# Layer 2's second block of gates and binary products as three rounded products each

## The reference, cut to what matters

```python
xn = _layernorm(x, axis=-1)
# L2_attn
i_raw, f_raw, g = xn @ Wi, xn @ Wf, xn @ Wg
i = silu(i_raw) * sigmoid(-f_raw)
a = exp(log_sigmoid(f_raw))
o = scan(a, i)                      # o[t] = a[t] * o[t-1] + i[t]
o = o * rsqrt(mean(o * o) + EPS) * g_norm_weight * silu(g)
# L2_ffn
bw = where(w >= 0, 1, -1) * mean(abs(w), per output row)
x = x + o @ Wo + xn @ bw.T + bias
```

## Time and profile before

| what | value |
|---|---|
| median of three runs | 674.25 us |
| the profiled execution's own time | 672.19 us |
| its span, first to last instruction | 670.4 us |
| TensorE matmul busy | 640.1 us, 95% |
| VectorE busy | 535.0 us, 80% |
| ScalarE busy | 344.5 us, 51% |
| GpSimd busy | 336.5 us, 50% |
| granted TensorE clock | 1.00 in every slice |

### The profile page before, as it was taken

The page is one execution under the profiler, slowest core; times in us unless marked ns, Lnnn a source line. Parts: engine busy times, 40 slices in busy tenths (PEclk is TensorE's granted clock), DMA queues, the critical chain, the costliest instruction groups (busy, mean ns, idle before and its releaser), DMA issues. The chain is left out here.

```text
span 670.4 us, 13518 instructions
## 1 busy us (share of the span) xinstructions
PE 640.1 (95%) x4850; PEld 502.5 (75%) x4850; DVE 535.0 (80%) x1080; ACT 344.5 (51%) x749; POOL 336.5 (50%) x267
## 2 busy tenths in 40 slices
PE   8998999999899999999999999999999999999887
PEld 3446887788478988889898788888877756767666
DVE  4378777698699898889899998668456889889993
ACT  1596211400556576664657555576436474379641
POOL 1063555592357667474875737978519633220000
PEclk9999999999999999999999999999999999999999
DMA  8801000000601001010010101100422200100001
GB/s 262 348 0 65 2 1 1 2 0 0 243 17 42 24 8 39 16 39 23 25 36 10 39 16 42 52 30 27 154 67 61 70 3 0 40 0 1 2 0 64
DMA packets 14792, 31.38 MB, mean 47 GB/s; under 512 B 1853, under 2 KB 8603, under 8 KB 14173
## 3 DMA queue, kind: packets, MB, share of 16 engines
q1 hardware_dynamic: 13069, 27.25, 12.1%
q0 software_dynamic: 1536, 3.15, 1.7%
q10 hardware_dynamic: 144, 0.40, 0.3%
HBM read 26.59 MB, written 5.24 MB: 47 GB/s over the span
## 5 line engine op out<-in xcount | busy, mean ns | idle before, releaser
L625 PE MATMUL bank<-zone 128*128 128x256 f32 (+1 forms) x472 | 166.8, 353 | 9.0 <-DVE arena L1778 2.7
L627 PE MATMUL bank<-zone 128*128 128x256 f32 (+1 forms) x472 | 156.1, 331 | 0.0
L626 PE MATMUL bank<-zone 128*128 128x256 f32 (+1 forms) x472 | 156.1, 331 | 0.0
L625 PEld LDWEIGHTS bank<-zone 128*128 128x128 f32 x472 | 88.7, 188 | 33.8 <-issue 12.2
L2274 POOL TENSOR_TENSOR arena<-arena 128x512 f32<-128x512 f32 x64 | 82.2, 1285 | 61.7 <-ACT arena L1351 61.6
L2279 POOL TENSOR_TENSOR arena<-arena 128x512 f32<-128x512 f32 x64 | 84.3, 1317 | 23.4 <-DVE arena L1778 13.0
L627 PEld LDWEIGHTS bank<-zone 128*128 128x128 f32 x472 | 88.8, 188 | 9.0
L626 PEld LDWEIGHTS bank<-zone 128*128 128x128 f32 x472 | 89.0, 189 | 5.3
L1370 ACT ACTIVATE arena<-arena 128x256 f32<-128x256 f32 (+1 forms) x128 | 62.1, 486 | 29.2 <-DVE arena L1787 28.6
L1787 DVE CUSTOM_DVE_ANT_0 arena<-bank,const 128x256 f32<-128x256 f32 (+1 forms) x128 | 45.6, 403 | 18.5 <-PE bank L821 17.5
L1803 DVE SCALAR_TENSOR_TENSOR x<-bank,arena,x 128x256 f32<-128x256 f32 x128 | 53.0, 473 | 7.7 <-PE bank L627 7.1
(11 more groups left out here) (299 smaller groups left out, 1340.2 us busy)
## 6 DMA issues: line engine op xcount, KB each, us to landing
arena<-in_qk SPq DMA_DIRECT2D x16, 256.0 KB
arena<-in_tern SPq DMA_DIRECT2D x1, 3072.0 KB, 20.9
arena<-in_wv SPq DMA_DIRECT2D x8, 256.0 KB, 2.8
arena<-in_wo SPq DMA_DIRECT2D x16, 128.0 KB, 2.0
arena<-in_wr SPq DMA_DIRECT2D x1, 1792.0 KB, 9.2
lB<-in_lB SPq DMA_DIRECT2D x1, 1288.5 KB, 23.6
xg_rows<-arena SPq DMA_DIRECT2D x1, 1024.0 KB
arena<-in_cossin SPq DMA_DIRECT2D x2, 512.0 KB, 4.7
```

Of the source, the lines that this page charges most:

```text
L625: pe.matmul(dst, lhi, rhi, start=(n == 0), stop=False)
L626: pe.matmul(dst, lhi, rlo, start=False, stop=False)
L627: last = pe.matmul(dst, llo, rhi, start=False, stop=(n == len(terms) - 1 and not open_end))
```

## The change

In layer 2, the six gate groups of block 1 and the binary products of token pairs 2 and 3 are computed as split products. Block 0 keeps its fp32 products.

- ScalarE gets a rounded copy of the three gate weights at once (128x1536) ahead of the ternary weights, and a rounded copy of bwT (128x512) ahead of the plain one. Its two copies of block 1's transposed tiles are rounded and go to xT3 and no longer to xT.
- VectorE gets two subtractions (rests of block 1, from PSUM) ahead of `recurrence(0)`, each behind a wait for ScalarE's copy. They give the semaphore on which TensorE's gates of block 1 wait.
- GpSimd gets four rests of 128x512: one of the gate weights ahead of the power of block 0, two behind it, and the one of bwT behind the power of block 1, ahead of the bias addition.
- TensorE waits for the rests of the weights (`rests2`) ahead of block 1's gates and ahead of the binary products of pairs 2 and 3.
- The arrays wg2 and bwT2 lie in memory of layer 1 that is no longer used. Two semaphores are new, two unused ones are gone.

```diff
+        bwT2 = [Carve(zone, z.at + 2 * BW + n * KD * D).grid(KD, D) for n in range(2)]
+        wg2 = [Carve(zone, ZONE - 6 * KD * D - 128 + n * 3 * KD * D).cols(3 * KD * D) for n in range(2)]
...
             def gate2(n, half, b):
-                base = B_W + (1, 0, 2)[n] * KD * D + half * P
-                wide(g_gate2[n][half][b], lambda k: lB[:, base + k * D:base + k * D + P], xT, b)
+                base = (1, 0, 2)[n] * KD * D + half * P
+                if b == 0:
+                    wide(g_gate2[n][half][b], lambda k: lB[:, B_W + base + k * D:B_W + base + k * D + P], xT, b)
+                    return
+                g = g_gate2[n][half][b]
+                reuse(g)
+                split_product(g.ps, [(cut(parts(wg2), ALL, slice(base + k * D, base + k * D + P)), cut(parts(xT3), ALL, k, slice(BW, T)))
+                                     for k in range(KD)]).then_inc(g.full_sem, 1)
...
             def project_ffn2(p):
-                tall(g_ffn2[p], p, lambda t: [(xT[:, k, tok(t)], bwT[:, k, :]) for k in range(KD)])
+                if p < 2:
+                    tall(g_ffn2[p], p, lambda t: [(xT[:, k, tok(t)], bwT[:, k, :]) for k in range(KD)])
+                    return
+                g = g_ffn2[p]
+                reuse(g)
+                for tt in range(2):
+                    last = split_product(g.ps[:, tt * D:(tt + 1) * D], [(cut(parts(xT3), ALL, k, tok(2 * p + tt)), cut(parts(bwT2), ALL, k)) for k in range(KD)])
+                last.then_inc(g.full_sem, 1)
...
                 pe.wait_ge(xT_ready, 4 * KD + KD * (b + 1))
+                if b:
+                    pe.wait_ge(rests2, 3)
...
             turn_ternary(range(4, len(g_wT3)))
+            pe.wait_ge(rests2, 4)
...
+            act.activation(wg2[0].bitcast(F32R), lB[:, B_W:B_W + 3 * KD * D], ACT.Copy).then_inc(rounded2, 1)
             keep_ternary(range(3))
             keep_xT(2, [0])
             keep_ternary([3])
             act.wait_ge(*g_bwT.full)
+            act.activation(bwT2[0].bitcast(F32R), g_bwT.ps.rearrange("p (k o) -> p k o", k=KD), ACT.Copy).then_inc(rounded2, 1)
             act.activation(bwT, g_bwT.ps.rearrange("p (k o) -> p k o", k=KD), ACT.Copy).then_inc(g_bwT.ready_sem, 1)
...
                         if (n, half, b) == (2, KD - 1, 0):
-                            keep_xT(2, [1])
+                            for k in range(KD):
+                                act.wait_ge(*g_xT[2][1][k].full)
+                                act.activation(xT3[0][:, k, BW:T].bitcast(F32R), g_xT[2][1][k].ps, ACT.Copy).then_inc(rounded2, 1)
...
+            for k in range(KD):
+                dve.wait_ge(rounded2, k + 3)
+                dve.tensor_tensor(xT3[1][:, k, BW:T].bitcast(F32R), g_xT[2][1][k].ps, xT3[0][:, k, BW:T], ALU.subtract).then_inc(xT_ready, 1)
             recurrence(0)
...
-            inverse_deviations(2)
-
+            def rest_of_wg2(n):
+                at = slice(n * KD * D, (n + 1) * KD * D)
+                rest([t[:, at] for t in wg2], lB[:, B_W + n * KD * D:B_W + (n + 1) * KD * D]).then_inc(rests2, 1)
+
+            pool.wait_ge(rounded2, 1)
+            rest_of_wg2(0)
+            inverse_deviation(2, 0)
+            rest_of_wg2(1)
+            rest_of_wg2(2)
+            inverse_deviation(2, 1)
+
+            pool.wait_ge(rounded2, 2)
+            pool.wait_ge(*g_bwT.ready)
+            rest(bwT2, bwT).then_inc(rests2, 1)
             pool.wait_ge(xn_ready, 3 * NT)
             pool.wait_ge(bias2_loaded, 16)
             pool.tensor_tensor(x, x, bias2.unsqueeze(1).to_broadcast([P, NT, D]), ALU.add).then_inc(bias2_added, 1)
```

More of the change, by code:

```diff
@@ L228, in build @@
         osq_summed = sem("osq_summed")
+        rounded2, rests2 = sem("rounded2"), sem("rests2")
         qk_full, v_full, wv_hi, wv_split = sem("qk_full"), sem("v_full"), sem("wv_hi"), sem("wv_split")
@@ L241, in build @@
             sem("idx_ready"), sem("rows_cleared"), sem("scattered"), sem("xg_loaded"), sem("combined"))
-        gathered = [sem(f"gathered{q}") for q in range(2 * NB)]
+        gathered = [sem(f"gathered{q}") for q in range(NB)]
         xg_act, xg_dve, y_act, y_dve, y_stored = sem("xg_act"), sem("xg_dve"), sem("y_act"), sem("y_dve"), sem("y_stored")
```

## The result

The changed kernel has a median of 676.84 us (675.88 to 678.26, eight runs) against 674.27 for the kernel before (672.1 to 675.65, eight runs): ratio 1.0044, interval 1.003 to 1.0059, some 2.6 to 3.0 us slower. The forecast was 677.8, in a range of 674.3 to 679.5.

The account below looks back on a forecast made before the run. VectorE and TensorE were taken to meet before layer 3, with VectorE later after the change. Rests (3.3 us) plus subtractions and product (0.3) delay it 3.6: 674.25 + 3.6 = 677.8 us, range 674.3 to 679.5.

Parts of the forecast that it names:

- The place and the mechanism: Layer 2's normalisations: GpSimd's rests queued behind the powers hold VectorE off through the shared port, making its chain late.
- Rival B: Layer 2's normalising instructions slip past GpSimd's rests without holds: +0.3 us, 674.5 us; chance 0.14.
- The size of a hold: Layer 2's normalisations: each of three GpSimd rests costs VectorE 1.1 us, 2.2 in block 0 and 1.1 in block 1.
- Rival A: Layer 2's normalisations: each rest holds VectorE for its whole spacing of 1.25 us, 0.45 more, 678.3 us; chance 0.12.
- The subtractions were hidden by the bias addition: Before layer 2's recurrence: VectorE's two subtractions (1.28 us) run during GpSimd's bias addition; 0.3 us of delay remains.
- the forecast picture: VectorE before layer 2's first scan: a gap of about 1 us, two subtractions, then a product of about 2.7 us.
- ScalarE's part: Rounding the gate weights after layer 1 costs some 1.5 us inside a 3.77 us gap; the binary-weight copy costs nothing.
- TensorE's part: Layer 2's gates save 2.0 us and binary products 0.7; the 2.7 us become idle time, 2 us before layer 3's transposes.
- Rival C: TensorE's list between 550.46 and 580 us sets the end, so its 2.7 us come back: 671.6 us; chance 0.12.
- its own condition: Before layer 3: it decides if VectorE is late by less than TensorE's saving of 2.7 us.
- 674.25 + 3.6: Whole kernel: median of the three runs shown plus the delay of VectorE's chain, giving 677.8 us.
- the line of 0.5%: Whole kernel: a measurement can tell about 0.5%, 3.4 us, from no change; same got 0.45, slower 0.49, faster 0.06.

## Why the prediction was right, and where it was off

**The place and the mechanism held.** The rests behind the powers hold VectorE off its normalisation. Removing them gives the time back, adding them alone costs it, and with them moved away both normalisations take 1.38 us again. The Trainium skill's rule (SBUF — State Buffer, "Who interferes with whom") says that VectorE and GpSimd share a port pair; the trace agrees, with 2.93 and 2.32 us against 1.38. Rival B, no holds, is out.

**The size of a hold was the term that was off.** "I take 1.1" for each of three rests, 3.3 us. Measured: 1.55 us for the two in block 0 and 0.94 for the one in block 1, 2.49 in all, or 0.78, 0.78 and 0.94 apiece. The price of 1.10 came from a product of 0.68 us that began with 1.24 us of a rest still to run (561.16 to 562.40) and ended 0.54 us behind it, so only 0.14 us of its own time passed beside the rest. Here the rests that read lB last 1.08 to 1.14 us and not 1.25, and a held instruction ends 0.14 to 0.16 us behind its rest, though a free one takes 0.40: some 0.25 us of its own time passes beside the rest. The rows of single instructions show the turns:

```profile
540.15 1.08 POOL L2263 TENSOR_TENSOR zone<-lB,zone 128x512 fp32r<-128x512 f32 x1
540.20 1.19 DVE L1622 TENSOR_SCALAR arena<-x,mv,lnw 128x256 f32<-128x256 f32 x1 [1.16 <-POOL lnw L2241]
541.20 1.14 POOL L2263 TENSOR_TENSOR zone<-lB,zone 128x512 fp32r<-128x512 f32 x1
541.30 1.18 DVE L1622 TENSOR_SCALAR arena<-x,mv,lnw 128x256 f32<-128x256 f32 x1
```

After each rest one normalising instruction gets through, then the next rest holds the next (541.30, behind 541.20). Rival A, the whole spacing of 1.25, which went the other way, is out. Why a rest from lB is shorter than one from the arena (1.26 at 551.86) was not tried.

**The subtractions were hidden by the bias addition**, as forecast: +0.42 us measured between the end of block 1's normalisation and the end of the first scan (554.25 to 560.74, against 549.52 to 555.59), 0.3 forecast; taking them away gave 0.43. The way there was not the one forecast in the recorded profile: a gap of about 1 us and a product of 2.7 us behind the addition were to be seen, but the slow clock stretched the gap to 3.35, and the subtractions ended at 558.89 against 558.87 for the addition, so the product ran free in 0.68. The two met there by chance. With the clock up the forecast picture is there, as in the run without rests:

```profile
558.61 1.29 DVE L2038 TENSOR_TENSOR zone<-bank,zone 128x512 fp32r<-128x512 f32 x2 [1.38 <-ACT zone L1499]
559.81 2.62 DVE L2019 TENSOR_TENSOR arena<-arena 128x512 f32<-128x512 f32 x1
```

With the filler ahead of layer 2 it is a gap of 1.05 and a product of 2.94. The sum is then 2.49 + 0.42 = 2.9 us, which is T's 2.96 and E's 2.86.

**ScalarE's part** cost nothing. Its rounding took 1.48 us (1.5 forecast) and lay in its idle time.

```profile
534.35 1.48 ACT L1480 ACTIVATE zone<-lB 128x1536 fp32r<-128x1536 f32 x1
```

**TensorE's part.** Six gate groups took 8.5 us (558.94 to 567.44; 8.4 forecast), and the saving did become a gap ahead of layer 3: 1.72 us in the run without rests and 1.73 in the one with the filler, 2 forecast. The run without rests tests Rival C by its own condition: VectorE was late by 0.4 us only, far less than TensorE's saving, and the time did not fall (1.0005). C is out, and so is its condition: in the kernel before it was already TensorE that waited for VectorE, 0.6 us in all. But C is closer to the truth than the text allowed: once the bias was shared in the kernel before, VectorE was the one that waited (0.81 us).

**What the text did not see** is the clock. It costed TensorE's waits as idle time alone. In the profile three of 0.7 us were followed by half speed for some 6 us. It did no harm here, as the run with the filler shows, because both what it delayed and the slack that it ate were covered by VectorE. In the kernel with the rests alone TensorE had no such slack, and the ratio was higher.

**The median.** 674.25 + 3.6 was forecast; 2.9 on top of it gives 677.15, and 676.84 was measured. The ratio of 1.0044 lies just under the line of 0.5%, on the side that got 0.45 and not 0.49; it was the larger hold that had put the forecast above it.

**A better version?** Sharing the bias addition on the kernel before gives 0.9979 (0.9959 to 0.9999), the lowest ratio of all, with an interval that ends just below 1. With the same sharing and the rests moved, the change itself leaves T 0.2 us shorter in the profiles (37.58 against 37.79), but its ratio is no lower (the intervals overlap), and the hold of the variances ahead of T's mark (0.58 us for 0.17 there too) takes 0.4 us back. In the kernel before with the shared bias TensorE is what VectorE waits for, so cheaper products do count there, but by these profiles they bring less than the wait for the subtractions and the hold of the variances take.

## What to carry to other kernels

Before giving GpSimd work "in its idle time", look at what VectorE issues in that moment: a rest of 128x512 behind a power cost 0.8 to 0.9 us each beside normalising instructions that work in SBUF, 0.4 us for two on a small write of variances, and nothing measurable beside additions that read PSUM. Where two engines meet at a point, making one cheaper only moves the idle time; see first which one arrives last, and by how much. A long blocked instruction (the scan of 5.43 us) is cover: what is put in front of it costs nothing until the cover is gone.

## What the runs showed of the hardware that was not expected

- Behind gaps of 0.7 us in a row TensorE ran at 0.50 of its clock for some us: the same 20 records took 11.44 us instead of 8.85. Behind one gap of 1.71 us it was granted 0.68 over 4 us. Behind gaps of 1.72 and 1.73 us two other profiles kept the full clock, so profiles of single executions differ by more than the changes under study.
- A matmul of one row and 256 columns in fp32 between matmuls of 128 rows cost 0.8 us.
- GpSimd and VectorE take turns instruction by instruction: a queue of two rests costs VectorE two holds, with one of its own instructions between them.
